# Tokens of the last six expert blocks summed on TensorE by one-hot products, in a one-core transformer layer with routed experts

## The reference

```python
h = tok(x, quantum_params, post_w, post_b)          # (8, 512, 192)
h = h + attention(layernorm(h))
g = layernorm(h)
top_scores, top_idx = top_k(g @ Wg, 2)              # two of eight experts
p = softmax(top_scores)
y = gelu(g @ W1[e] + b1[e]) @ W2[e] + b2[e]         # 192 -> 384 -> 192
h = h + p[0] * y[top_idx[0]] + p[1] * y[top_idx[1]]
```

## Time and profile before

| | |
|---|---|
| median of three runs | 297.35 us (296.71 to 297.77) |
| span of the profiled execution | 294.9 us |
| what lies around the span (median less span) | 2.45 us |
| busy: PE / PEld / DVE / ACT / POOL | 72% / 51% / 59% / 41% / 71% |
| chain that ended last: PE / DVE / POOL / issue / ACT / DMA | 47% / 21% / 12% / 7% / 7% / 4% |
| scatters of results, L770 | 71, 72.6 us busy |
| down products, L2096 | 426 records, 81.0 us busy |

### The profile page before, as it was taken

The page is one execution under the profiler, slowest core; times in us unless marked ns, Lnnn a source line. Parts: engine busy times, 40 slices in busy tenths (PEclk is TensorE's granted clock), DMA queues, the critical chain, the costliest instruction groups (busy, mean ns, idle before and its releaser), DMA issues.

```text
span 294.9 us, 5764 instructions
## 1 busy us (share of the span) xinstructions
PE 211.9 (72%) x1552; PEld 150.7 (51%) x1552; DVE 175.2 (59%) x687; ACT 121.3 (41%) x292; POOL 210.2 (71%) x281
## 2 busy tenths in 40 slices
PE   0760699367864678977689598999999999988000
PEld 0540554122431434544356387878789989867000
DVE  5754999756899989595887757784211000842122
ACT  2002013135351331356533467667665766745000
POOL 5777786740899697877776776777777777777750
PEclk9999999655596655579855779999999999999655
DMA  7811003994000000000012221022333315997454
GB/s 166 278 18 15 1 3 118 397 328 163 2 0 0 4 9 11 13 13 17 14 22 47 60 45 26 16 85 86 100 101 89 96 67 175 370 364 234 111 222 161
DMA packets 25659, 29.86 MB, mean 101 GB/s; under 512 B 15130, under 2 KB 19473, under 8 KB 25435
## 3 DMA queue, kind: packets, MB, share of 16 engines
q1 hardware_dynamic: 19148, 21.54, 23.3%
q0 software_dynamic: 6480, 7.94, 8.8%
HBM read 14.13 MB, written 16.02 MB: 102 GB/s over the span
## 4 chain that ended last, share of the span: by engine, by line
PE 47%; DVE 21%; POOL 12%; issue 7%; ACT 7%; DMA 4%; POOLq 1%; DVEq 0%; SPq 0%; ACTq 0%
PE bank_b L2096 24%; PE bank_a L2084 6%; POOL circuit L542 5%; PE bank_b L1855 4%; PE bank_a L1862 3%; POOL shares_out L770 3%; DVE nmax L1191 3%; POOL rs L714 2%; PE bank_c L1874 2%; ACT prob L1593 2%; POOL routed L725 1%; DMA angle_stages<-shares_out 1%; PE bank_d L1958 1%; DVE circuit L883 1%; DMA shares_out<-circuit,up 1%
## 5 line engine op out<-in xcount | busy, mean ns | idle before, releaser
L770 POOL DMA_INDIRECT shares_out<-circuit,up x71 | 72.6, 1023 | 21.6 <-issue 16.5
L2096 PE MATMUL bank_b<-wide,up 128*128 x426 | 81.0, 339 | 2.8 <-ACT up L1720 1.2
L725 POOL DMA_INDIRECT routed<-rows,slot x64 | 63.3, 989 | 23.5 <-issue 18.9
L2096 PEld LDWEIGHTS bank_b<-wide,up 128*128 128x128 f32 x426 | 69.7, 194 | 9.9 <-issue 8.3
L1732 ACT ACTIVATE circuit<-bank_b,up 128x192 f32<-128x192 f32 x71 | 29.9, 421 | 25.0 <-PE bank_b L2096 23.4
L542 POOL DMA_INDIRECT circuit<-angles,ids x32 | 31.3, 978 | 10.8 <-issue 9.0
L1720 ACT ACTIVATE up<-bank_a 128x384 f32<-128x384 f32 x71 | 34.5, 489 | 6.9 <-PE bank_a L2084 6.9
L1862 PE MATMUL bank_a<-keys_t,wt 32*128 32x512 f32 x64 | 27.8, 956 | 4.7 <-DVE nmax L1191 3.0
L1855 PE MATMUL bank_b<-queries_t,keys_t 32*128 32x512 f32 x64 | 24.6, 850 | 6.2 <-ACT keys_t L1571 3.5
L1518 DVE TENSOR_TENSOR hres<-hres,prob 128x384 f32<-128x384 f32 x12 | 6.2, 559 | 37.8 <-DMA prob<-shares_out 37.7
L1191 DVE TENSOR_REDUCE nmax<-bank_a 128x2 f32<-128x1024 f32 x16 | 19.5, 1220 | 11.3 <-PE bank_a L1862 11.3
(11 more groups left out here) (433 smaller groups left out, 392.9 us busy)
## 6 DMA issues: line engine op xcount, KB each, us to landing
routed<-pad_rows SPq DMA_DIRECT2D x8, 528.0 KB, 5.2
out<-hres SPq DMA_DIRECT2D x7, 384.0 KB, 6.0
wide<-down_w SPq DMA_DIRECT2D x1, 2304.0 KB, 12.6
prob<-shares_out SPq DMA_DIRECT2D x3, 768.0 KB, 5.4
up<-up_w SPq DMA_DIRECT2D x1, 1536.0 KB
angle_stages<-shares_out SPq DMA_DIRECT2D x2, 768.0 KB, 7.0
form_p<-shares_out SPq DMA_DIRECT2D x2, 768.0 KB, 7.1
up<-routed SPq DMA_DIRECT2D x71, 16.0 KB, 1.7
```

Of the source, the lines that this page charges most:

```text
L725: pool.indirect_dma_start(out=routed, out_offset=bass.IndirectOffsetOnAxis(slot[:, b, k, j:j + 1], 0), in_=rows[:, b, k, j, :], in_offset=None
L770: pool.indirect_dma_start(out=shares_out, out_offset=bass.IndirectOffsetOnAxis(xb[:, m, DEST:DEST + 1].bitcast(I32), 0), in_=y[:, m % RESU ...
L2096: mm = pe.matmul(bank_b[:, m % 2, 0:D], hid[:, m % STEP, c * P:(c + 1) * P], wide_flat[:, bass.ds(first + c * D, D)], start=(c == 0), stop ...
```

## The change

The results of the last six blocks (65 to 70, `LOCAL = 6`) are no longer scattered. DVE compares the token addresses of these blocks with the addresses of batch 7, which POOL writes once as 512 numbers, and makes for each block a 128x512 matrix with a one where row and token belong together (`pick_rows`). PE multiplies it with the block's result (`unite`): four products of 128x128 by 128x192 for each block, summed over the six blocks in the free columns of `bank_c` and `bank_d`. DVE adds these sums to `hres` after the two share rows of batch 7. Rows of `shares_out` that nobody now writes must read as zero, so `hres` of batch 7 is cleared at the start and stored over both share rows. SP waits for 65 blocks, not 71, before it loads batch 7, and the store of batch 6 now stands behind these loads.

```diff
+    LOCAL = 6
+    SENT = BLOCKS - LOCAL
...
             sp.dma_start(wide[:, :, 0:HC * D], down_w.rearrange("p (e x) -> p e x", e=E)).then_inc(down_in, 16)
+            sp.wait_ge(zeros_ready, 1)
+            sp.dma_start(shares_view[BATCHES - 1], hres[:, BATCHES - 1, :].unsqueeze(1).to_broadcast([P, 2, TILES * D])
+                         ).then_inc(zeros_out, 16)
             sp.wait_ge(up_copied, E)
...
-            for b in range(BATCHES - 1 - SUMS, BATCHES - 1):
+            for b in range(BATCHES - 1 - SUMS, BATCHES - 2):
                 store(b)
-            all_added(sp, BLOCKS)
+            all_added(sp, SENT)
             for x in range(2):
                 load_last_half(x)
+            store(BATCHES - 2)
             for x in range(2):
                 store_last_half(x)
...
                 step(pool.iota(exp_i[:, :], [[1, E]], base=0, channel_multiplier=0))
+                pool.wait_ge(lifted_done, 1)
+                pool.iota(local_i[:, :, :], [[1, TILES], [TILES, P]], base=(BATCHES - 1) * SEQ, channel_multiplier=0
+                          ).then_inc(local_ready, 1)
...
-            for m in range(BLOCKS):
+            pool.wait_ge(zeros_out, 16)
+            for m in range(SENT):
                 pool.wait_ge(y_done, m + 1)
...
             dve.memset(ones[:, :], 1.0).then_inc(ones_done, 1)
+            dve.memset(hres[:, BATCHES - 1, :], 0.0).then_inc(zeros_ready, 1)
...
-                dve.tensor_tensor(hres[:, b, own], hres[:, b, own], sums[:, 1, own], ALU.add).then_inc(sum_done, 1)
+                step(dve.tensor_tensor(hres[:, b, own], hres[:, b, own], sums[:, 1, own], ALU.add))
+                join()
+                dve.wait_ge(united, x + 1)
+                here = bank_d[:, P:P + TILES // 2 * D] if x else bank_c[:, 0:TILES // 2 * D]
+                dve.tensor_tensor(hres[:, b, own], hres[:, b, own], here, ALU.add).then_inc(sum_done, 1)
+
+            def pick_rows():
+                dve.wait_ge(local_ready, 1)
+                dve.wait_ge(exp_done, 2 * BATCHES)
+                for s in range(SENT // STEP, STEPS):
+                    dve.wait_ge(block_in[s], 16 * len(blocks_of(s)))
+                step(dve.tensor_scalar(dest_i[:, :, :], xb[:, SENT:BLOCKS, DEST:DEST + 1].bitcast(I32), TOKENS - 1, None,
+                                       ALU.bitwise_and))
+                join()
+                step(dve.tensor_copy(dest_f[:, :].unsqueeze(2), dest_i[:, :, :]))
+                join()
+                for n in range(LOCAL):
+                    dve.tensor_scalar(picks[n], local_i[:, :, :].rearrange("p j t -> p (j t)"), dest_f[:, n:n + 1], None,
+                                      ALU.is_equal).then_inc(picks_done, 1)
...
             for s in range(LOADED_STEPS, STEPS):
                 expert_up(s)
+            pick_rows()
             for b in range(BATCHES - 1):
                 add_experts(b)
...
+            def unite(m):
+                n = m - SENT
+                pe.wait_ge(picks_done, n + 1)
+                pe.wait_ge(y_done, m + 1)
+                if n == 0:
+                    pe.wait_ge(h2_copied, 2 * BATCHES)
+                    pe.wait_ge(xt_copied, STEPS)
+                for j in range(TILES):
+                    first = j % 2 * D
+                    into = bank_d[:, P + first:P + first + D] if j >= 2 else bank_c[:, first:first + D]
+                    mm = pe.matmul(into, picks[n][:, j * P:(j + 1) * P], y[:, m % RESULTS, :], start=(n == 0),
+                                   stop=(m == BLOCKS - 1), skip_group_check=True)
+                    if m == BLOCKS - 1 and j % 2 == 1:
+                        mm.then_inc(united, 1)
...
                 tail(m)
+                if m - 1 >= SENT:
+                    unite(m - 1)
+            unite(BLOCKS - 1)
```

More of the change, by code:

```diff
@@ L255, in build @@
         xt = sb("xt", [P, 1, P])
+        local_i = wqkv0[:, 0:SEQ].bitcast(I32).rearrange("p (j t) -> p j t", j=TILES)
+        dest_i = sb("dest_i", [P, LOCAL, 1], I32)
+        dest_f = sb("dest_f", [P, LOCAL])
         xb = behind(up_room, "p (m f) -> p m f", m=BLOCKS, f=F)
@@ L266, in build @@
                     "p (k x) -> p k x", k=2)]
+        spread_room = u_rep[:, :, :, :, :].rearrange("p a j g f -> p (a j g f)")
+        picks = [keys_t[:, n, :] for n in range(3)] + [queries_t[:, :]] + [
+            spread_room[:, n * SEQ:(n + 1) * SEQ] for n in range(2)]
         bank_a = ctx.enter_context(nc.psum_tensor("bank_a", [P, TILES, 512], F32))
@@ L368, in build @@
         passed = sem("passed")
+        zeros_ready = sem("zeros_ready")
+        zeros_out = sem("zeros_out")
+        local_ready = sem("local_ready")
+        picks_done = sem("picks_done")
+        united = sem("united")
         def blocks_of(s):
@@ L476, in load_last_half @@
                 b = BATCHES - 1
+                if x == 0:
+                    sp.wait_ge(sum_done, b - SUMS + 1)
                 sp.dma_start(expert_sums[b % SUMS][:, :, own], shares_view[b][:, :, own]).then_inc(last_in[x], 16)
@@ L1601, in h2_copy @@
                 rows_of = hres[:, b, 2 * h * D:2 * (h + 1) * D]
+                if b == BATCHES - 1:
+                    act.wait_ge(zeros_out, 16)
                 if b >= HALF:
```

## The result

| | before | after |
|---|---|---|
| median of the first runs (µs) | 297.03 (294.94 to 297.77, 4 runs) | 292.54 (291.69 to 294.01, 4 runs) |
| ratio, 95% interval | | 0.9881 [0.9834, 0.9928] |
| median of the repeat, another set of runs (µs) | 296.71 (17 runs) | 294.41 (291.64 to 296.08, 12 runs) |
| ratio, 95% interval | | 0.9918 [0.9885, 0.9951] |
| span of the profiled execution (µs) | 294.9 | 290.0, repeat 292.4 |

The ratio is the record's estimate from the runs, not the quotient of the two medians (0.985 and 0.992). One of the 12 runs of the repeat, at 296.08, is in the chip's slower state and is left out of the ratio.

The account below looks back on a forecast made before the run. POOL's scatter backlog, then load, adds and store, was taken to set the end. Adds start 290.41 - 5.7, plus 3.40 for adds and 2.28 behind them: span 290.4; with 2.45, median 292.85, said as 292.8; range 291.2 to 295.0 (8 in 10).

Parts of the forecast that it names:

- Six scatters less: End of POOL's row: block 64's scatter becomes the last, 7.73 µs earlier, six at 1.29; batch 7 loadable from 279.2.
- the slip: POOL's later scatters all shift by 0.36 µs, as three scatters beside DVE's comparisons take 0.12 longer each.
- The load now meets other traffic: SP's queue: batch 7's load stands behind batch 6's load and two stores; its adds start at 284.7, 5.7 µs earlier.
- its upper bound: Latest start of batch 7's adds, 285.1: block 64's scatter takes 5.65 µs to the load's issue, then 3.39.
- the first rival: Block 64's scatter lands last of all, 7.5 µs, under batch 6's load: adds at 287.3, time 295.4; chance 0.07.
- Two adds more: DVE's end: each half of batch 7 has three adds in sequence, adding 1.2 µs (0.6 to 2.4).
- PE's work: 24 one-hot products at 0.37 µs, 8.8 in all; PE ends at 280.7, last `unite` 281.3; hidden with 4.6 cover.
- both rivals on the clock: PE at its lower clock: in `unite` alone, time 295.5, chance 0.05; from block 65 on, 301.9, chance 0.03.
- DVE's one-hot matrices: Six comparisons and two small ones, 2.9 µs, hidden in DVE's idle time; POOL slowed 0.36 (bounds 0 and 2.9).
- The port rule: DVE's two-port instructions block POOL: comparisons cost it up to 2.9 µs; rival with time 295.0 or a little over, chance 0.05.
- Small work early: Memset, POOL's address list and zeros written to DRAM cost nothing; rival: zeros delay angle gathers 2.05 µs, 294.9, chance 0.04.
- What lies around the span: Frame added to each profiled span to get the median time: 2.45 µs, from 297.35 against 294.9.

Follow-up runs that it names:

- sums first: Changed kernel with the PSUM sums added to batch 7's rows before batch 6's adds; 292.20 µs, 0.9848 of the kernel before.
- both: Changed kernel with the PSUM sums added early and batch 7's loads ahead of the stores of batches 4 to 6; 292.85 µs, 0.9873 of the kernel before.
- scatter first: Changed kernel with PSUM sums added early and SP holding batch 6's load until POOL issued the last scatter; 291.77 µs, 0.9857 of the kernel before.
- 8 blocks: Changed kernel with LOCAL = 8 instead of 6 and two more one-hot buffers, 63 blocks scattered; 292.64 µs, 0.9891 of the kernel before.
- loads first: Changed kernel with batch 7's loads ahead of the stores of batches 4, 5 and 6 in SP's queue; 293.58 µs, 0.9894 of the kernel before.
- five blocks: Changed kernel with LOCAL = 5 instead of 6, 66 blocks scattered; 295.86 µs, 1.0003 of the kernel before.
- Products twice: Changed kernel with every one-hot product done twice, 24 more products on PE; 294.54 µs, 0.9954 of the kernel before.
- small load: Changed kernel with batch 6's load cut to 96 of 768 columns; 291.22 µs, 0.9861 of the kernel before.

## Why the prediction came out right, step by step

**The bound** was named right: in the kernel before POOL's backlog, then load, adds, store. After it, the last scatter is off the end of the chain in one execution, and on it in the other.

**Six scatters less.** Forecast 7.73 less 0.36 for the slip, with some 0.4 given back. From first to last scatter it is 92.72 before, 85.81 after and 85.07 in the repeat: 6.91 and 7.65. The second is the forecast; the first execution lost 0.7 on the way, inside what the eight executions with 65 scatters span, 85.07 to 86.61.

**The load now meets other traffic: the step that was mis-sized.** Forecast: adds from 284.7, 5.7 earlier. Against the first result scatter they begin at 99.35 before, 95.03 after, 96.09 in the repeat: 4.3 and 3.3 earlier. The working itself held where the last scatter is issued in time: 8.19 from batch 6's load to the adds (284.7 - 276.51), measured 8.24, and 7.8 to 9.2 in the four others of that order (sums first, both, scatter first, 8 blocks). What it missed is, in the first execution, that batch 6's load itself was issued 86.79 after the first result scatter where it was 85.45 before, 1.34 of drift and slip; and in the repeat, the scatter's late landing, which makes that 8.19 into 10.53. There the adds wait for their DMA until 286.72, past the 286 that the prediction had named as a sign of being wrong, and past its upper bound, which took 5.65 for the scatter and 3.39 for the load: measured are 6.23 to the load's issue and 4.70 to its landing.

This is the first rival, given 0.07: it put the adds 10.9 behind the last scatter and the time at 295.4; the repeat shows 11.02 and a median of 294.41. Its sum came out by luck, since its terms, 7.5 and 3.39, are off in opposite directions. It is no mishap of one scatter but depends on how far ahead of batch 6's load the scatter starts. I argued against it from the DMA share of 0.25 at the scatter's start, when the load that matters was issued 0.46 later. The trace of the kernel before held the answer. Asked for this scatter alone (start 276.05), it gives the landing, and for the queues from 277.1 to 280 one line, with no packet of a scatter in it:

```profile
DMA to landing us min/median/max: 5.7/5.7/5.7
...
q1 hardware_dynamic: 152, 0.47, 79.7%
```

That landing harmed nothing there, as six more scatters followed. Of five profiled executions with 65 scatters, the whole load, the products done once and the order left to itself, three went the early way and two the late way (repeat, loads first). Which share of all executions goes which way is open: a run without a profile doesn't tell.

**Two adds more.** 1.2 forecast, 3.39 - 2.21 = 1.18 measured, and given back when they were moved.

**PE's work.** 0.37 a product forecast, 0.325 measured (eight in 2.60); PE ended at 277.79, not 281.3, with the granted clock at 1.00; 1.8 of that is the middle's. In the repeat the clock stands at 1.00 up to PE's end too, so both rivals on the clock are out for these executions.

**DVE's one-hot matrices.** In DVE's and POOL's timelines of the changed kernel:

```profile
234.27 0.17 DVE L1569 TENSOR_SCALAR dest_i<-up 128x6 int32<-128x6 int32 x1 [12.07 <-DMA up<-routed]
...
234.75 1.39 DVE L1575 TENSOR_SCALAR keys_t<-wqkv,dest_f 128x512 f32<-128x512 int32 x3
...
234.51 0.99 POOL L794 DMA_INDIRECT shares_out<-circuit,up  x1 [0.30 <-ACT circuit L1779]
235.80 1.25 POOL L794 DMA_INDIRECT shares_out<-circuit,up  x1 [0.30 <-ACT circuit L1779]
```

They run while DVE would be idle, 3.05 µs from 234.27 to 237.32, and one of two scatters beside them is 0.27 longer (forecast 0.36). In each of the eleven executions with comparisons one or two scatters beside them took 1.13 to 1.27; of the scatters with an idle DVE beside them none in any trace took over 1.00. POOL was slowed, and did not stand still.

The port rule of the Trainium skill, "SBUF — State Buffer", section "Who interferes with whom", would have cost up to 2.9 (an estimate) if the comparisons ran in one of the two-port modes that it speaks of; no run shows in which mode they ran. By the trace the effect is a tenth of that.

**Small work early.** Timelines of DVE and POOL after:

```profile
7.00 0.55 DVE L831 TENSOR_REDUCE lift_sum<-lift 128x2 f32<-128x384 f32 x1 [1.29 <-DMA wg<-gate_w]
...
69.44 0.25 DVE L856 TENSOR_SCALAR angle_stages<-circuit 128x150 f32<-128x150 f32 x1 [0.54 <-DMA circuit<-angles,ids]
...
71.54 1.22 DVE L1216 TENSOR_REDUCE nmax<-bank_a 128x2 f32<-128x1024 f32 x1 [0.22 <-PE bank_a L1909]
...
28.42 0.59 POOL L753 IOTA wqkv<- 128x512 int32 x1
```

The waits of the earlier trace rows took in the memset and the list. The last reduction of angles stands at 69.44, 0.59 late, with a wait for its gather that was not there before. That the zeros held the gather up is likely and not shown: the same wait (0.31 to 0.54) stands in three of the twelve executions that write zeros, in none of the other nine and in neither without them. DVE's next wait, on PE, swallowed it (0.22 instead of 0.84), so it costs nothing.

**What lies around the span** was taken as 2.45, a median less the span of one execution. Runs that list both mostly have some 1.7 (291.69 and 290.0 in the profiled one). Against the profiled run's 291.69 the forecast of 292.8 was 1.1 too high, in parts that partly cancel: a tail that came out 1.4 longer, against a frame 0.76 too large and a middle that happened to be 1.8 early. That it lies so near the median of 292.54 is luck. The 0.3% that the forecast took for the least difference to be told from none was too small: the intervals here reach 0.3% to 0.6% to either side.

## What to carry to other kernels

Work taken from the front of a chain pulls its tail forward only until the tail meets the transfer ahead of it; count the gain from that transfer's issue, not from the work removed. Where a small indirect DMA and a large load are issued within a microsecond of each other, ask which one's packets go first, and look up that very DMA's landing in the trace you have: here the answer stood in the trace of the kernel before. With five blocks the late landing and the two more adds took back what the missing scatters gave; with six a gain was left in either order. And a sum that is ready early should be added early: two adds moved into idle time of DVE shorten the tail by 1.2 µs, beside the 2.1 to 3.1 of the whole change.

## What the runs showed of the hardware that was not expected

**A scatter beside a load.** How long a scatter of 128 rows takes to land goes by how far ahead of batch 6's load (786 KB) it starts. Started 0.23 to 0.62 µs ahead, it landed 4.4 to 5.8 after its start (seven executions, among them all three with 71 scatters); 0.78 to 1.33 ahead, 2.3 to 2.6 (four executions); the scatter before that, 1.75 to 2.9 ahead, 2.3 to 2.6 (twelve). Started 0.68 to 1.1 behind the load, it took 6.6 to 6.8 (five). Products twice stands between: 3.9 at 1.57, with two of its 32 data packets left when the load's began. With an eighth of the load, 0.22 ahead, it took 2.7. That the scatter's packets stand behind the load's is shown by the packet records and by the small load; the order itself was forced once each way (five blocks, and scatter first). At batch 4's load, which comes while others still run, scatters 1.0 to 1.4 ahead took 5.2 to 7.0, so the figures are for batch 6's load alone.

**A load's slow start.** With no store among it (loads first), batch 6's load moved 71 GB/s in the microsecond from 278, 258 in the next and 416 in the third, at DMA shares of 0.58, 0.77 and 1.03. With stores among it, the windows of the changed kernel above show 158 at 1.03 and 215 at 0.79, and 398 at 283 to 284. Why the first packets take so long is open.
